# First cross attention of a six-layer stack: split q and k packed through DRAM for float32r score matmuls

## The chip, the cores and the metric

One core of a Trainium2 chip. The metric is the device time of the whole kernel in microseconds, the median of the runs shown.

## The reference, cut to what matters

64 sequences of 128 tokens and 128 channels pass through six layers: windowed attention, **cross attention with a memory**, routed experts, narrow attention, cross attention over pairs and a quantised feed-forward. Each layer adds its input and normalises. The change lies in the second layer:

```python
q = x @ Wq + bq                        # 128 x 128, 16 heads of 8
k = concat([fside @ Wk + bk, ctx])     # 128 + 120 keys
v = concat([fside @ Wv + bv, ctx])
attn = softmax(q k^T * 8 ** -0.5)      # per head, 128 x 248
out = (attn v) @ Wp + bp
x = layernorm(x + out)
```

(The reference concatenates the projected keys with `ctx_1024`; the kernel handles the 120 rows of `ctx_1024` and the 128 projected rows as two blocks of keys.)

## The kernel before, in words

The layers are stages in time, one block of engine programs each, with all engines meeting between them: `attend_window` (0 to about 478 us), `attend_keys_major` (478 to about 1130), `experts_sparse`, `attend_narrow`, `attend_pairs`. Everything here concerns `attend_keys_major`.

**Steps.** `pipeline` unrolls the first and last steps and loops over the middle. Step c works on sequences at different depths: SP loads for c+4 and c+3; PE transposes x and projects q, k, v for c+2 (`a`); ACT copies q and k out for c+1 (`b`), and POOL multiplies q with `quadmask` into `Qm` (L1732); PE computes the scores of c; the keys-major scores, exponentials and weighted sums belong to c-1 and c-2; c-3 to c-6 finish (normalisation, transposes, stores into `routed_x`, `routed_xT` and the logits). Most tiles are rings of four.

**The scores.** 16 heads lie as four groups of 32 partitions with four heads of 8 channels in each. To multiply one head with a 32-row contraction, `Qm` holds q four times, with only one head's channels kept in each copy. Scores are computed twice. In L1478 and L1489 ("across": queries by 248 keys, in banks S) they serve only the row maxima, which DVE takes with negation (L1625). In L1473 ("down": keys by four heads times 128 queries, 512 columns, in banks T) they get the negated maxima added by a bfloat16 matmul from `NB` (L1485), and ACT exponentiates them (L1577). `weigh` (L1504) multiplies with V, 32 small matmuls a call. Float32 matmuls appear in the trace as two passes each, so L1473 has two PE instructions for each line executed.

**Order on PE in step c**, which is written out by hand: `scores(c,0)`, `weigh(c-2,0)`, the transposes of the maxima through `diag` (L1523), `scores(c,1)`, transposes of x, xo and O (L1531, L1537, L1539, L1544), `scores(c,2)`, `weigh(c-2,1)`, `scores(c,3)`, transposes of OT and the projections (L1550, L1551, L1560 to L1564). Each call of `scores` is a round: two groups of down, two groups of across, on four different row groups, then two NB matmuls. Three banks each for S and T are reused within a step: round 1 needs the bank whose maxima DVE took in round 0.

**Other engines.** DVE, in order: normalisation of O (L1638 to L1645), V (L1414, L1415), y (L1656), two maxima, statistics, the copy of NB (L1665), two maxima, logits (L1675), xoT (L1679), oT (L1687), two maxima, xo (L1693), two maxima. ACT: q, k, two exponentials of 512 columns in each round, the copies of xT (L1598) and OT (L1603). POOL: the split of the maxima into three bfloat16 parts (L1719 to L1727), Qm, the context part of V (L1411, L1412), the power (L1742), yb (L1746). SP issues the seven transfers of a step in order (L1432 to L1449), with waits between them; it is one queue.

The stage before it ends with `slots<-blank` stores (L369, L389) that zero a DRAM area for the experts stage; before the change the stage doesn't wait for their landing.

Of the kernel before, what the change touches and what calls it, by code (L numbers as in the profile page):

```python
# [16 lines left out]
F32 = mybir.dt.float32  # L17
BF16 = mybir.dt.bfloat16
U32 = mybir.dt.uint32
# [4 lines left out]
P = 128  # L24
CTX = 120
WH = 8
# [14 lines left out]
BLANKS = 8  # L41

# [38 lines left out]
def looped(at):  # L81
    return not isinstance(at.p, int)

# [52 lines left out]
def allocate(K):  # L136
# [8 lines left out]
    K.alibi = K.sb("alibi", [P, WH * 48])  # L145
# [7 lines left out]
    K.blank = K.sb("blank", [P, BLANKS, ROW])  # L153
    K.half = K.sb("half", [P, 2])
    K.eps = K.sb("eps", [P, 1])
    K.Mself = K.sb("Mself", [P, WH * P])
    K.Nself = K.sb("Nself", [P, WH * P])
    K.Gram = K.sb("Gram", [P, 2 * P])
# [14 lines left out]
    K.tstep = K.sb("tstep", [P, 3])  # L173

# [84 lines left out]
def late_loads(K, D):  # L259

    return [
        (K.xw[:, 0, :], D["L0_xattn_Wq"]), (K.xw[:, 1, :], D["L0_xattn_Wk"]),
        (K.xw[:, 2, :], D["L0_xattn_Wv"]), (K.xw[:, 3, :], D["L0_xattn_Wp"]),
        (K.xb[:, 0:1], D["L0_xattn_bq"].rearrange("(d a) -> d a", a=1)),
        (K.xb[:, 1:2], D["L0_xattn_bk"].rearrange("(d a) -> d a", a=1)),
# [19 lines left out]
def attend_window(K, D, tag, x_dram, out_dram, nseq):  # L285
# [14 lines left out]
    with ExitStack() as ctx:  # L300
# [53 lines left out]
        with nc.Block() as block:  # L354
            @block.sync
            def _(sp):
# [972 lines left out]
def attend_keys_major(K, D, tag, x_dram, routed, nseq):  # L1329
# [6 lines left out]
    places = (slice(0, CTX), slice(CTX, CTX + P))  # L1336
# [6 lines left out]
    with ExitStack() as ctx:  # L1343
# [3 lines left out]
        def sem(name):  # L1347
# [6 lines left out]
        xf = [sb(f"xf{i}", [P, 2 * P + CTX + P]) for i in range(ring)]  # L1354
        qT = [sb(f"qT{i}", [P, P]) for i in range(2)]
        Qm = [sb(f"Qm{i}", [P, J * P]) for i in range(ring)]
# [24 lines left out]
        f_in = [sem(f"f_in{i}") for i in range(ring)]  # L1381
        xT_out = [sem(f"xT_out{i}") for i in range(ring)]
# [7 lines left out]
        cleared, ready, masked, put_ctx, split, maxed = (sem(n) for n in (  # L1390
            "cleared", "ready", "masked", "put_ctx", "split", "maxed"))
# [6 lines left out]
        cT, kT = slice(2 * P, 2 * P + CTX), slice(2 * P + CTX, 2 * P + CTX + P)  # L1398
        every = slice(2 * P, 2 * P + CTX + P)
# [24 lines left out]
        with nc.Block() as block:  # L1424
            @block.sync
            def _(sp):
                def step(c):
                    a, l, s, o = c + 4, c + 3, c, c - 5
                    if a.live:
# [3 lines left out]
                        sp.dma_start(cx[a.slot][0:CTX, :], D["ctx_1024"][a.n]).then_inc(x_in[a.slot], 16)  # L1433
                    if s.live:
# [11 lines left out]
                    if l.live:  # L1446
                        need(sp, T_ps, (l - 4).done(2 * R, 4))
# [120 lines left out]
            def _(act):  # L1568
# [11 lines left out]
                def step(c):  # L1580
# [11 lines left out]
                    if a.live:  # L1592
                        need(act, in_ps, a.done())
                        if n.live:
                            need(act, oT_ps, n.done())
# [656 lines left out]
```

## Time and profile before

| | us |
|---|---|
| runs (3) | 2698.47, 2702.93, 2707.09 |
| median | 2702.93 |
| profiled execution, span from first to last instruction | 2695.8 |
| profiled execution, its own time outside the span | not listed apart; the runs are 2.7 to 11.3 above the span |
| instructions | 95989 |
| PE busy in the span | 2502.7 (93%) |
| DVE, ACT, POOL busy | 1849.6, 1737.7, 1401.1 |

How to read it: PE is TensorE's matmuls and PEld its weight loads, DVE is VectorE, ACT ScalarE, POOL GpSimd, SP the engine that issues transfers (SPq its issues). The busy time of PE is an average over five stages. One step of the stage at hand is the time between two equal instructions of the loop.

### The profile page before, as it was taken

To read this page: it belongs to the slowest core of one execution; us is meant where nothing else is said; L and a number is where in the kernel's file an instruction comes from. 1 tells how busy PE (TensorE), PEld (TensorE's weight loads), DVE (VectorE), ACT (ScalarE), POOL (GpSimd) and SP (SyncE) were. 2 spreads that over 40 slices of the span, in tenths; PEclk is the share of its full clock that TensorE was granted. 3 is DMA by queue.
4 is the path that set the end of the run, shared out by engine and by line. 5 is a ranking of instruction groups with operands and counts; after the bars stand their busy time and mean duration, and the time that the engine had idled before them with its cause. 6 is when DMAs were issued, how large, how long until landed. Compare 5 with 4: busy or idle time off the path is not lost. (4 is left out here: it accounts for less than half of the span.)

```text
span 2695.8 us, 95989 instructions
## 1 busy us (share of the span) xinstructions
PE 2502.7 (93%) x29950; PEld 2007.2 (74%) x29951; DVE 1849.6 (69%) x5434; ACT 1737.7 (64%) x6375; POOL 1401.1 (52%) x2914
## 2 busy tenths in 40 slices
PE   7999999799999999788889969999999799999995
PEld 6888888577777777487667758888888688888883
DVE  4565555588888888564334448888887388888886
ACT  4666666355555555213556638888888588888883
POOL 2333333233444344165774447777776266666664
PEclk9999999799999999899999979999999899999997
DMA  6332322211111111123332211111111111111100
GB/s 158 100 88 79 89 81 65 65 49 48 49 48 48 48 47 44 37 85 84 78 80 66 66 48 53 47 53 49 50 53 37 33 31 32 31 31 31 31 26 11
DMA packets 270161, 151.37 MB, mean 56 GB/s; under 512 B 51776, under 2 KB 263744, under 8 KB 270016
## 3 DMA queue, kind: packets, MB, share of 16 engines
q1 hardware_dynamic: 261312, 131.57, 18.2%
q0 software_dynamic: 8704, 17.97, 1.9%
q8 instruction: 78, 1.28, 0.2%
q14 instruction: 67, 0.55, 0.1%
HBM read 92.52 MB, written 48.51 MB: 52 GB/s over the span
## 5 line engine op out<-in xcount | busy, mean ns | idle before, releaser
L1187 ACT ACTIVATE pr<-psS,small 128x128 f32<-128x128 f32 x1024 | 366.7, 384 | 95.9 <-DVE small L1258 94.0
L1625 DVE TENSOR_REDUCE small<-psS 128x2 f32<-128x496 f32 x512 | 321.4, 669 | 90.3 <-PE psS L1489 89.1
L1577 ACT ACTIVATE pr<-psT 120x512 f32<-120x512 f32 (+1 forms) x384 | 215.1, 595 | 136.9 <-PE psT L1485 124.5
L1473 PE MATMUL psT<-cross_Qm,cross_xf 32*120 32x512 f32 (+1 forms) x768 | 292.1, 641 | 0.5 <-ACT pr L1577 0.2
L1187 ACT ACTIVATION_READ_ACCUMULATOR pr<-psS,small 128x1 f32 x1024 | 226.1, 221 | 0.0
L1478 PE MATMUL psS<-cross_xf,cross_Qm 32*128 32x248 f32 x1024 | 209.1, 428 | 1.1 <-DVE small L1625 1.1
L2172 POOL DMA_INDIRECT results<-experts_ob,experts_xb x144 | 138.5, 962 | 115.4 <-ACT experts_ob L1992 100.5
L1258 DVE TENSOR_REDUCE small<-psS 128x8 f32<-128x1024 f32 x128 | 156.7, 1224 | 60.5 <-PE psS L1152 60.3
L2112 DVE SCALAR_TENSOR_TENSOR experts_bgh<-experts_bth,psS 128x256 f32<-128x256 f32 x144 | 60.7, 421 | 198.9 <-ACT experts_bth L1984 198.9
L956 POOL TENSOR_SCALAR pr<-pr,small 128x120 f32<-128x120 f32 x512 | 180.4, 372 | 23.3 <-DVE small L910 23.3
L814 ACT ACTIVATE pr<-psS,small 128x120 f32<-128x120 f32 x512 | 179.0, 391 | 5.0 <-DVE small L929 5.0
L1489 PE MATMUL psS<-cross_xf,cross_Qm 32*128 32x248 f32 x1024 | 181.4, 376 | 0.0
L484 ACT ACTIVATE pr<-pr,small 128x48 f32<-128x48 f32 x512 | 166.9, 331 | 2.9 <-DVE small L551 2.9
L1111 PE MATMUL psT<-ident,pr 128*128 128x128 f32 x1024 | 161.6, 281 | 0.2
L1152 PEld LDWEIGHTS psS<-self_qk,self_Qm 32*128 32x128 f32 x2048 | 125.7, 188 | 45.9 <-issue 45.9
L2163 POOL DMA_INDIRECT slots<-routed_x,experts_idx x128 | 123.6, 965 | 66.7 <-issue 38.1
L470 ACT COPY self_Y<-psW 128x512 f32<-128x512 f32 x128 | 68.7, 589 | 126.8 <-PE psW L456 126.8
L1152 PE MATMUL psS<-self_qk,self_Qm 32*128 32x128 f32 x2048 | 150.3, 285 | 0.0
L1473 PE MATMUL psS<-cross_Qm,cross_xf 32*120 32x512 f32 (+1 forms) x256 | 143.9, 642 | 0.0
L1504 PEld LDWEIGHTS psW<-pr,cross_Vx 120*32 120x32 f32 (+1 forms) x4096 | 104.0, 109 | 52.7 <-issue 51.8
L583 POOL TENSOR_TENSOR small<-small,eps 128x1 f32<-128x1 f32 x64 | 12.2, 191 | 249.0 <-DVE small L517 249.0
L1577 ACT ACTIVATE pr<-psS 120x512 f32<-120x512 f32 (+1 forms) x128 | 76.1, 595 | 98.9 <-PE psT L1485 98.9
(323 smaller groups left out, 8058.1 us busy)
## 6 DMA issues: line engine op xcount, KB each, us to landing
self_parts<-results SPq DMA_DIRECT2D x64, 192.0 KB, 2.4
slots<-blank SPq DMA_DIRECT2D x18, 520.0 KB, 4.5
experts_xb<-slots SPq DMA_DIRECT2D x144, 65.0 KB, 1.9
self_near<-in_x SPq DMA_DIRECT2D x128, 64.0 KB, 1.9
between<-self_xo SPq DMA_DIRECT2D x128, 64.0 KB, 1.6
cross_x<-between SPq DMA_DIRECT2D x128, 64.0 KB, 1.8
cross_res<-between SPq DMA_DIRECT2D x128, 64.0 KB, 1.8
self_x<-in_x SPq DMA_DIRECT2D x64, 64.0 KB, 1.8
```

Of the source, the lines that this page charges most:

```text
L484: last = act.activation(head(pr[e.slot], h), head(pr[e.slot], h), ACT.Exp, bias=nmax[e.slot % 2][:, h:h + 1], accum_out=tot[e.slot][:, h:h ...
L814: last = act.activation(pr[b.slot][:, i * P:i * P + CTX], S0[:, i * P:i * P + CTX], ACT.Exp, bias=nmax[b.slot % 2][:, i:i + 1], accum_out= ...
L956: last = pool.tensor_scalar(pr[w.slot][:, i * P:i * P + CTX], pr[w.slot][:, i * P:i * P + CTX], inv[w.slot][:, i:i + 1], 1.0, ALU.mult, AL ...
L1111: last = pe.transpose(W[half][:, n * P:(n + 1) * P], pr[t.slot % 4][:, (4 * half + n) * P:(4 * half + n + 1) * P], K.ident[:])
L1152: last = pe.matmul(K.S[u.slot % 2][:, 512 * half + m * P:512 * half + (m + 1) * P], Qm[i.slot % 2][rows(g), m * P:(m + 1) * P], qk[i.slot] ...
L1187: last = act.activation(pr[e.slot % 4][:, cols], K.S[e.slot % 2][:, cols], ACT.Exp, bias=nmax[e.slot % 4][:, n:n + 1], accum_out=tot[k.slo ...
L1258: dve.tensor_reduce(nmax[u.slot % 4][:], src, AX.X, ALU.max, negate=True).then_inc(maxed, 1)
L1473: pe.matmul(to[0:size, :], xf[t.slot][rows(g), every][:, places[ck]], Qm[t.slot][rows(g), :], start=True, stop=False)
L1478: pe.matmul(to[:, 0:CTX + P], Qm[c.slot][rows(g), P * j0:P * j0 + P], xf[c.slot][rows(g), every], start=True, stop=True)
L1489: pe.matmul(to[:, 256:256 + CTX + P], Qm[c.slot][rows(g), P * j0 + P:P * j0 + 2 * P], xf[c.slot][rows(g), every], start=True, stop=True).t ...
L1577: act.activation(PT[k][0:sizes[ck], 512 * n:512 * n + 512], T[turn[2 * r + n]][0:sizes[ck], :], ACT.Exp).then_inc(exped, 1)
L1625: dve.tensor_reduce(nmax[c.slot % 2][:, J * sg[n] + j0:J * sg[n] + j0 + 2], src, AX.X, ALU.max, negate=True).then_inc(maxed, 1)
```

## The change

What it does:

- q and k get a channel order by place in the head group (`t_xq`, `t_xk`, `t_bq`, `t_bk`, `t_ctxq` prepared on the host). ACT writes q and k, and a transfer the context, into `low` (128 x 376). DVE keeps the upper bits in `high` (one `bitwise_and` over 376 columns), POOL subtracts `high` from `low`.
- SP stores high and low in four transfers to a DRAM tensor `parts` (four combinations of high and low q with high and low k), waits for all of them to land, and loads `pack` (128 x 4 x 376) from it. In `pack` the 32 rows of a group hold, for each of four heads, 8 channels in the four combinations. `Qm`, `qT`, `quadmask`'s multiply and the load of `t_ctx` are gone.
- The scores read `pack` as float32r: across is still two matmuls of 248 columns a group and round, down is four of 128 columns with weights of their own in place of one of 512.
- NB, xoT, oT and the logits are copied by ACT, xo is computed by POOL; DVE did all five.
- Projections run one step earlier (a = c+3), q and k are copied out at h = c+2; V's projection is at c+2.
- `keep_awake` issues unread 512-column float32 matmuls: six before the first wait of the stage, and in the unrolled steps up to sequence 1 two or six at the start of a step and one in its middle.
- The stage before now waits for all `slots<-blank` stores, and some of its tiles are freed at its end.

Core of the diff:

```diff
 (SP)
-                    if l.live:
-                        need(sp, T_ps, (l - 4).done(2 * R, 4))
-                        sp.dma_start(xf[l.slot][:, P:2 * P], D["t_fside"][l.n]).then_inc(f_in[l.slot], 16)
-                        sp.dma_start(xf[l.slot][:, cT], D["t_ctx"][l.n]).then_inc(f_in[l.slot], 16)
+                        need(sp, v_ps, (a - 4).done())
+                        sp.dma_start(xf[a.slot][:, P:2 * P], D["t_fside"][a.n]).then_inc(f_in[a.slot], 16)
+                    if l.live:
+                        need(sp, parts_out[(l - 2).slot], (l - 2).p * STORES + STORES)
+                        sp.dma_start(low[l.slot % 2][:, 2 * P:], D["t_ctxq"][l.n]).then_inc(c_in[l.slot], 16)
...
+                    if h.live:
+                        need(sp, low_sb, h.done())
+                        to = K.parts[h.slot].rearrange("n p k -> p n k")
+                        mine = part[h.slot % 2]
+                        sp.dma_start(to[:, 0:4:3, :], mine[:]).then_inc(parts_out[h.slot], 16)
+                        sp.dma_start(to[:, 1:3, queries], mine[:, :, queries]).then_inc(parts_out[h.slot], 16)
+                        sp.dma_start(to[:, 1, keys], mine[:, 1, keys]).then_inc(parts_out[h.slot], 16)
+                        sp.dma_start(to[:, 2, keys], mine[:, 0, keys]).then_inc(parts_out[h.slot], 16)
+                        need(sp, T_ps, (h - 4).done(2 * R))
+                        need(sp, parts_out[h.slot], h.p * STORES + STORES)
+                        sp.dma_start(pack[h.slot][:].rearrange("p j k -> p (j k)"),
+                                     K.parts[h.slot].rearrange("n (s j) k -> s n (j k)", j=J)).then_inc(
+                            pack_in[h.slot], 16)
 (PE)
+                wide = K.xw[:, 0:4, :].rearrange("p n d -> p (n d)")
+                keep_awake(pe, W1, K.ident[:], wide, 6)
...
+                    def down(n, j):
+                        if t.live:
+                            g, to = tg[n], T[turn[2 * r + n]]
+                            pe.matmul(to[0:size, P * j:P * j + P], pack[t.slot][rows(g), j, places[ck]].bitcast(F32R),
+                                      pack[t.slot][rows(g), j, queries].bitcast(F32R), start=(j == 0), stop=False)
+                    def across(n, j):
+                        if c.live:
+                            g, to = sg[n], S[turn[2 * r + n]]
+                            last = pe.matmul(to[:, 256 * j:256 * j + CTX + P], pack[c.slot][rows(g), j0 + j, queries].bitcast(F32R),
+                                             pack[c.slot][rows(g), j0 + j, keys].bitcast(F32R), start=True, stop=True)
...
-                            pe.matmul(to[0:size, :], xf[t.slot][rows(g), every][:, places[ck]], Qm[t.slot][rows(g), :],
-                                      start=True, stop=False)
...
+                    filling = not looped(c) and c.n < 2
+                    if filling and not c.live:
+                        keep_awake(pe, W1, K.ident[:], wide, 2)
+                    if filling and c.live and not m.live:
+                        keep_awake(pe, W1, K.ident[:], wide, 6)
...
+                    if filling:
+                        keep_awake(pe, W1, K.ident[:], wide, 1)
 (DVE, at the start of a step, ahead of the first maxima)
+                    if h.live:
+                        need(dve, qk_sb, h.done(2))
+                        need(dve, c_in[h.slot], h.landed())
+                        need(dve, parts_out[c.slot], c.p * STORES + STORES)
+                        dve.tensor_scalar(high[h.slot % 2].bitcast(U32), low[h.slot % 2].bitcast(U32), UPPER, None,
+                                          ALU.bitwise_and).then_inc(top_sb, 1)
 (POOL)
-                        pool.tensor_tensor(Qm[b.slot][:].rearrange("p (j q) -> p j q", j=J),
-                                           qT[b.slot % 2][:].rearrange("p (j q) -> p j q", j=1).to_broadcast([P, J, P]),
-                                           K.quadmask[:].rearrange("p (j q) -> p j q", q=1).to_broadcast([P, J, P]),
-                                           ALU.mult).then_inc(masked, 1)
+                    if h.live:
+                        need(pool, top_sb, h.done())
+                        pool.tensor_tensor(low[h.slot % 2], low[h.slot % 2], high[h.slot % 2],
+                                           ALU.subtract).then_inc(low_sb, 1)
 (stage before, SP)
+                sp.wait_ge(K.emptied, 16 * empty.shape[0])
```

## Rows read from the trace of the kernel before

**Rows 1.** Page: the span.

```profile
span 2695.8 us, 95989 instructions
```

**Rows 2.** Windows: filling, then steady steps: length; PE, PEld, DVE, ACT, POOL; clock, DMA share, GB/s.

```profile
480.00:540.00 60.00, 53.54 (x509) 37.28 (x510) 33.82 (x88) 20.88 (x49) 16.08 (x47) 0.75 0.18 43
...
560.00:656.50 96.50, 96.50 (x1428) 68.42 (x1427) 79.27 (x228) 55.98 (x124) 39.23 (x116) 1.00 0.18 49
```

**Rows 3.** Instruction groups, forms apart, 560 to 1090 us: busy, mean ns, idle.

```profile
L1625 DVE TENSOR_REDUCE small<-psS 128x2 f32<-128x496 f32 x448 | 281.0, 669 | 69.4 <-PE psS L1489 68.9
...
L1577 ACT ACTIVATE pr<-psT 128x512 f32<-128x512 f32 x168 | 93.9, 594 | 31.8 <-PE psT L1485 31.8
L1732 POOL TENSOR_TENSOR cross_Qm<-cross_qT,quadmask 128x512 f32<-128x512 f32 x56 | 58.3, 1041 | 0.1
...
L1665 DVE CAST cross_NB<-psW 128x512 bf16<-128x512 f32 x56 | 38.7, 691 | 4.2
```

**Rows 4.** Timeline of PE over one step: start us, us, instruction.

```profile
706.44 0.69 PE L1473 MATMUL psT<-cross_Qm,cross_xf 32*120 32x512 f32 x1
...
707.79 1.08 PE L1504 MATMUL psW<-pr,cross_Vx 128*32 128x128 f32 x32
...
708.80 0.69 PE L1473 MATMUL psT<-cross_Qm,cross_xf 32*120 32x512 f32 x1
...
710.08 0.33 PE L1550 MATMUL psW<-ident,cross_OT 128*128 128x128 f32 x1
...
711.34 0.69 PE L1473 MATMUL psT<-cross_Qm,cross_xf 32*128 32x512 f32 x1
...
712.62 1.08 PE L1504 MATMUL psW<-pr,cross_Vx 120*32 120x128 f32 x32
...
713.63 0.40 PE L1523 MATMUL psW<-identb,cross_diag 128*128 128x128 bf16 x4
...
713.96 0.69 PE L1473 MATMUL psS<-cross_Qm,cross_xf 32*128 32x512 f32 x1
...
715.24 0.33 PE L1531 MATMUL psW<-ident,cross_x 128*128 128x128 f32 x1
```

**Rows 5.** Timeline of PE inside the round from 713.96: second pass, then NB.

```profile
714.49 0.59 PE L1473 MATMUL psS<-cross_Qm,cross_xf 32*128 32x512 f32 x1
...
714.92 0.37 PE L1485 MATMUL psS<-cross_NB,cross_onesb 32*128 32x512 bf16 x1
```

**Rows 6.** Timeline of PE: float32 matmuls of 128 columns, two passes each.

```profile
710.35 0.39 PE L1560 MATMUL psW<-cross_xf,xw 128*128 128x128 f32 x2
...
710.58 0.39 PE L1561 MATMUL psW<-cross_xf,xw 128*128 128x128 f32 x2
```

**Rows 7.** Timeline of SP: first and last of a step's seven issues.

```profile
710.24 0.34 SPq L1448 DMA_DIRECT2D cross_xf<-in_t_fside  x1
...
713.56 0.51 SPq L1444 DMA_DIRECT2D routed_x<-cross_xo  x1
```

**Rows 8.** DMA issues: count, KB each, median us from issue to landing.

```profile
slots<-blank SPq DMA_DIRECT2D x18, 520.0 KB, 4.5
...
between<-self_xo SPq DMA_DIRECT2D x128, 64.0 KB, 1.6
...
wT<-in_t_wq SPq DMA_DIRECT2D x1, 512.0 KB, 3.6
```

**Rows 9.** Windows of one us around the stage's start, columns as in Rows 2.

```profile
474.00:475.00 1.00, 0.00 (x0) 0.00 (x0) 0.00 (x0) 0.00 (x0) 0.00 (x0) 0.50 1.02 377
...
482.00:483.00 1.00, 0.00 (x0) 0.00 (x0) 0.62 (x17) 0.00 (x0) 0.25 (x2) 0.50 0.92 204
```

**Rows 10.** Timeline of the filling: stage's first memset, first scores, third sequence's.

```profile
478.12 0.91 DVE L1610 MEMSET cross_Vx<- 128x1024 f32 x1 [6.13 <-PEq L354]
...
489.48 1.20 PE L1478 MATMUL psS<-cross_xf,cross_Qm 32*128 32x248 f32 x4
...
511.95 0.69 PE L1473 MATMUL psT<-cross_Qm,cross_xf 32*128 32x512 f32 x1
```

More of the change, by code:

```diff
@@ L17 @@
 F32 = mybir.dt.float32
+F32R = mybir.dt.float32r
 BF16 = mybir.dt.bfloat16
@@ L82, in looped, with keep_awake @@
     return not isinstance(at.p, int)
+def keep_awake(pe, bank, weights, moving, times):
+    for _ in range(times):
+        pe.matmul(bank, weights, moving, start=True, stop=True)
 def pipeline(eng, step, ring, count, first, lo, hi, last):
@@ L173, in allocate @@
     K.tstep = K.sb("tstep", [P, 3])
+    K.alibi = K.sb("alibi", [P, WH * 48], F32, early)
+    K.Mself = K.sb("Mself", [P, WH * P], F32, early)
+    K.Nself = K.sb("Nself", [P, WH * P], F32, early)
+    K.Gram = K.sb("Gram", [P, 2 * P], F32, early)
+    K.blank = K.sb("blank", [P, BLANKS, ROW], F32, early)
 def set_up(K, D):
@@ L1352, in attend_keys_major @@
         res = [sb(f"res{i}", [P, P]) for i in range(ring)]
-        xf = [sb(f"xf{i}", [P, 2 * P + CTX + P]) for i in range(ring)]
-        qT = [sb(f"qT{i}", [P, P]) for i in range(2)]
-        Qm = [sb(f"Qm{i}", [P, J * P]) for i in range(ring)]
+        xf = [sb(f"xf{i}", [P, 2 * P]) for i in range(ring)]
+        part = [sb(f"part{i}", [P, 2, WIDE]) for i in range(2)]
+        high, low = ([v[:, i, :] for v in part] for i in range(2))
+        pack = [sb(f"pack{i}", [P, J, WIDE]) for i in range(ring)]
         Vx = [sb(f"Vx{i}", [P, 2, G, P]) for i in range(ring)]
@@ L1381, in attend_keys_major @@
         f_in = [sem(f"f_in{i}") for i in range(ring)]
+        c_in = [sem(f"c_in{i}") for i in range(ring)]
+        parts_out = [sem(f"parts_out{i}") for i in range(ring)]
+        pack_in = [sem(f"pack_in{i}") for i in range(ring)]
+        top_sb, low_sb, v_ps = sem("top_sb"), sem("low_sb"), sem("v_ps")
         xT_out = [sem(f"xT_out{i}") for i in range(ring)]
@@ L1389, in attend_keys_major @@
             "in_sb", "qk_sb", "v_sb", "nb_sb", "exped", "O_sb", "oT_sb"))
-        cleared, ready, masked, put_ctx, split, maxed = (sem(n) for n in (
-            "cleared", "ready", "masked", "put_ctx", "split", "maxed"))
+        cleared, ready, put_ctx, split, maxed = (sem(n) for n in (
+            "cleared", "ready", "put_ctx", "split", "maxed"))
         inverted, scaled = sem("inverted"), sem("scaled")
@@ L1553, in step @@
                         need(pe, in_sb, a.done())
-                        need(pe, f_in[a.slot], a.p * 32 + 32)
+                        need(pe, f_in[a.slot], a.landed())
                     if n.live:
@@ L1596, in step @@
[L1596 to L1597 removed]
                         act.copy(xf[a.slot][:, 0:P], W0[:, 0:P]).then_inc(in_sb, 1)
+                    if n.live:
+                        need(act, y_ps, (n - 2).done())
+                        act.copy(oT[n.slot % 2][:], W0[:, 384:512]).then_inc(oT_sb, 1)
+                    if v.live:
+                        act.copy(routed.logits[:, bass.ds(v.n, 1), :].rearrange("p a e -> p (a e)"), W0[:, 256:256 + EXPERTS])
@@ L1599, in step @@
+                    if z.live:
+                        need(act, xT_out[z.slot], (z - 4).landed())
+                        act.copy(xoT[z.slot][:], W0[:, P:2 * P]).then_inc(turned_sb, 1)
                     exps(c, 2)
@@ L1742, in step @@
                         pool.tensor_tensor(rs[w.slot % 2][:], ve[w.slot % 2][:], K.half[:, 0:1], ALU.pow).then_inc(lnroot, 1)
+                        need(pool, lnroot, w.done())
+                        need(pool, stored[w.slot], (w - 4).landed())
+                        need(pool, turned_ps, (w - 4).done())
                     if v.live:
```

139 lines of the change are left out of this document (65 added, 74 removed).

## The prediction

> **What bounds the kernel now.** I read the windows first. In a stretch of 96.5 us (10.2 steps of 9.46) PE is busy 96.50 of 96.50 us at full clock, DVE 79.27, ACT 55.98, POOL 39.23, and DMA 18% at 49 GB/s [rows 2]. The reader is to see that in the steady part only PE has no slack. The groups give the step: 448 maxima, eight a step, are 56 steps in 530 us, 9.46 us each [rows 3]. The timeline of PE cuts that step. Three rounds of scores take 1.28 us and one 1.35 (706.44 to 707.79), in all 5.19. The rest is two `weigh` of 1.01, diag 0.33, the transposes 0.66 (715.24 to 706.44 plus one step) and the tail 1.26 from 710.08 to 711.34: 4.27, and 9.46 with the rounds [rows 4]. The change attacks the 5.19. The stage fills from 478.12, computes its first scores at 489.48 and those of the third sequence at 511.95 [rows 10], at a mean clock of 0.75 [rows 2].
>
> **PE after the change.** A round's first pass starts at 713.96, the second 0.53 later, NB 0.43 after that, and the next work 0.32 later [rows 4, 5]. So a 512-column float32 pass streams in 0.43, with 0.10 to start a round. The four row groups run side by side, so the down groups, which also carry NB, set the length; across is two matmuls of 248 columns and fits beside them. New is: 0.10 + four matmuls of 128 columns with weights of their own + 0.32 for NB and the turn to the next work. No row has float32r. The nearest below is bfloat16: four diag matmuls of 128 columns in 0.33, 0.083 each [rows 4]. The nearest above that is one float32 pass: L1560's two passes take 0.23, some 0.11 each [rows 6]. The far end is both passes, 0.22 to 0.23. The round is 0.75, 0.86 or 1.32 us, and the step on PE 4.27 + 4 x round = 7.3, 7.7 or 9.5. I take one float32 pass, 7.7, because the operands are 32 bits wide and it is one pass.
>
> **The other engines.** DVE sheds NB, 0.69 [rows 3], and four smaller copies, and gains one bitwise operation over 376 columns ahead of its first maxima: from 7.77 a step (79.27 / 10.2 [rows 2]) it stays below 7.7 even if that costs 0.6, NB alone counted. It delays the first maxima; round 1 of PE needs their bank, and may wait some 0.3 us, so PE stands near 8.0. ACT gains NB (about the 0.59 of an exponential of the same size [rows 3]) and three copies, together about 1.3: 5.5 [rows 2] becomes 6.8. POOL, 3.85 [rows 2], loses 1.04 for Qm's 512 columns [rows 3] and gains a subtraction over 376 and xo over 128, each less than that: under 4.9. So these cost nothing while PE or SP takes 7.7 us or more.
>
> **SP and the transfers.** This is the new path. Per step SP issues seven small transfers as before (x, cx, fside, ctxq, res, xT, xo), then waits for POOL's `low`, issues four stores of 752 KB together, waits until they have landed, and issues the 752 KB load. Nothing passes the wait: x, fside and the next sequence's stores are queued behind it. The seven issues take 3.83 us today, from 710.24 to 714.07 [rows 7]. The pack's issue is another 0.5. The landing: a 64 KB store to DRAM takes 1.6, 512 KB inward 3.6, and 520 KB of blanks 4.5 in a busy stretch [rows 8]; full engines moved 377 GB/s [rows 9]. From the first issue, 1.6 + 688 KB at 377 GB/s (1.9) is 3.5 at the low end; by the blanks' slope, 2.9 us for 456 KB, it is 1.6 + 4.4 = 6.0 at the high end. I take 4.0, nearer the low one, because the rows stored here are mostly 1 to 1.5 KB long and the engines are else little used. So SP's turn is 3.83 + 4.0 + 0.5 = 8.3 us, with ends of 7.8 and 10.3. The load itself has a step and a half until it is needed, so its 3 to 4 us are hidden; if SP falls behind, that cover is gone and SP's turn is the step. 1.5 MB more per step at 377 GB/s is 4.1 us of 8.3: the engines are not full.
>
> The Trainium skill ("DMA: Bandwidth & Descriptors", Anatomy of one DMA) fits a transfer on its GpSimd path as about 2.0 us plus bytes over 436 GB/s, most of the fixed part being the receipt from the target. By that the stores would land 3.8 us after the first issue, SP's turn would be 8.1 and the total below 13 us lower; no row here shows it for this queue.
>
> **Step and steady gain.** The step is the longest of PE 8.0 and SP 8.3: 8.3. Over some 62 steps (64 less the filling) 62 x (9.46 - 8.3) = 72 us saved. The drain has score work too: 2 us more.
>
> **Filling.** First, the stage before now waits for its blank stores. DMA engines are still 92% busy up to 483 [rows 9], where the stage had begun at 478.12 [rows 10]: up to 4.9 us later. Second, the unread matmuls stand ahead of the first transpose: six of two passes are 5.2 us warm (12 x 0.43) and 10.3 at half clock. Third, the first scores now wait for copy, split, stores and load, about 8 us more. I expect first scores some 18 us later than 489.48. But the next steps were slow before, 22.5 us for two (489.48 to 511.95 [rows 10]), and come at SP's pace, 16.6, from there, some at full clock. The third sequence starts about 12 us later than before; less 3 for what the blanks would have delayed anyway, 9. Bounds are 3 and 18.
>
> Sum: 72 + 2 - 9 = 65 us off the span of 2695.8 [rows 1], 2631. The median of the runs shown stands 7.1 above that span, so **2638**.
>
> **The rivals.**
> 1. *The round trip is shorter and PE decides* (chance 0.20). SP issues at its best and the stores land in 3.5; DVE's wait stays hidden. PE's row-based 7.3 to 7.7 sets the step, say 7.5: 62 x 1.96 + 2 - 9 = 115, 2588. For it: a load's issue itself takes 0.34 [rows 7], and at 0.45 from issue to issue SP's turn is 3.2 + 3.5 + 0.5 = 7.2. Against: the spacing is 0.55 today (3.83 / 7), and the stage has DVE waits within a step.
> 2. *float32r at short columns is no cheaper than two float32 passes*, so that the change doesn't do what it says (0.08). No matmul here has 256 columns. The round is 1.32, the step 9.5, and only the filling remains: 2703 + 7, some 2710. For it: no row excludes it. Against: one pass issued in place of two.
> 3. *Slower: SP waits for its stores longer than 5.1 us.* That is the point at which its turn reaches 9.46. At the blanks' slope the landing is 6.0, the step 10.3: 62 x 0.84 + 7 = 59 more, 2762 (0.12). For it: 520 KB took 4.5 [rows 8], four stores plus a write receipt each step, and the loads in flight share the engines. Against: the blanks are 520-byte rows beside a stage at up to twice this stage's traffic.
> 4. *A step of 8.8 to 9.4*, the same mechanism short of the turning point (0.10): 2670 to 2706.
>
> **How the numbers follow.** The forecast, a step of 7.9 to 8.8, has 0.50, and its own range is 2613 to 2669. About 0.3% (8 us, 2695 to 2711) is what a measurement here can tell from no change. Faster takes the forecast, rival 1 and most of rival 4, 0.79. Within: most of rival 2 and the edge of rival 4, 0.07. Slower: rival 3 and the rest of rival 2, 0.14. The range of 2582 to 2706 takes in rival 1 and rival 4 and leaves out rival 3 and most of rival 2.
>
> **What would show it.** In the trace after: L1473's successor with one PE instruction a matmul, four in 0.33 to 0.46; rounds near 0.86; PE under 100% busy in steady steps, and its idle time ended by the landing of `pack` if SP decides, by DVE's maxima at round 1 if it doesn't. SP's own queue should wait 2 us after the fourth store. The steps between equal maxima should be 8.3. DMA share should rise from 0.18 to above 0.6. The first scores should stand 15 to 20 us later. The prediction is wrong if float32r matmuls of 128 columns start 0.2 us apart, if the stores land after 5.1 us, or if the step is set by ACT, whose copies now stand between its exponentials.

## The result and the profile after

The change makes the kernel slower: 2821.34 us median of four runs (2802.70 to 2857.34) against 2700.70 before, a ratio of 1.0424 with a 95% interval of 1.0386 to 1.0462. The prediction was 2638 (2582 to 2706). The profiled execution took 2802.7 us, its span is 2800.9, against a span of 2695.8 before [rows 1]. Ratios in this document leave out runs over 1.5% above the fastest of their kernel (here 2857.34), so they differ a little from the quotient of the medians.

The page of the kernel after: the span, then PE's busy tenths, the granted clock and the DMA share in 40 slices of 70 us.

```profile
span 2800.9 us, 96503 instructions
PE   7999997999999999869888987999999799999995
PEclk9999999768755557989999998999999999999997
DMA  6323232566644445622333221111111111111100
```

The reader is to see the clock's row: from the 8th to the 16th slice, all of them in the first cross attention, it stands at 5 to 8 tenths, while PE's row shows 9 tenths busy in every one. PE is not short of work there, it runs at half clock. The windows of the stage say it more closely (length; PE, PEld, DVE, ACT and POOL busy; clock, DMA share, GB/s):

```profile
660.00:699.00 39.00, 38.82 (x697) 29.77 (x696) 32.35 (x91) 31.93 (x81) 22.96 (x60) 1.00 0.70 214
700.00:730.00 30.00, 25.89 (x471) 19.92 (x471) 21.92 (x60) 20.64 (x52) 15.36 (x40) 1.00 0.71 225
760.00:1060.00 300.00, 300.00 (x3072) 223.21 (x3068) 147.46 (x397) 145.34 (x353) 100.88 (x264) 0.50 0.47 149
```

These are the three paces of the stage, where before there was one [rows 2]. I take the pace from the distance between POOL's subtractions, one a step. From 660 to 699 PE is full at full clock: 7.76 us a step. From 700 to 730 PE is 86% busy at full clock: 8.5 to 9.6 us. From 760 to 1060 PE is full at 0.50, which is 1.2 GHz: 13.6 us. In this execution 33 steps behind the first scores take 12.8 us or more, in stretches of 2, 5 and 26 (the first 2 are in the filling, where the kernel before had slow steps too).

Between the second and the third pace stands this, in windows of 2 us:

```profile
726.00:728.00 2.00, 0.46 (x8) 0.28 (x7) 0.94 (x6) 0.66 (x3) 1.25 (x5) 1.00 1.02 360
728.00:730.00 2.00, 2.00 (x54) 1.47 (x51) 1.29 (x3) 1.09 (x2) 0.85 (x1) 1.00 0.78 262
...
736.00:738.00 2.00, 1.20 (x22) 0.97 (x26) 0.79 (x4) 0.44 (x3) 0.71 (x3) 0.95 0.82 245
738.00:740.00 2.00, 2.00 (x36) 1.50 (x28) 1.51 (x4) 0.90 (x2) 1.34 (x3) 0.50 0.98 331
```

and in the timeline of PE the wait that empties the first of them:

```profile
727.73 0.32 PE L1502 MATMUL psT<-cross_pack 32*128 32x128 f32 x1 [1.54 <-DMA cross_pack<-parts]
```

PE stands for `pack` 1.54 us before 727.73 and again 1.34 before 736.80; then the clock is at half. The earlier fall, at about 588, has a wait of 1.53 us before 585.76 in front of it.

SP's own timeline shows why `pack` is late (one turn, from pack load to pack load; L1472 and L1475 are the first and last store, L1478 the load):

```profile
723.27 0.57 SPq L1478 DMA_DIRECT2D cross_pack<-parts  x1
724.18 0.34 SPq L1449 DMA_DIRECT2D cross_x<-between  x1
...
727.38 0.50 SPq L1466 DMA_DIRECT2D routed_x<-cross_xo  x1
727.99 0.52 SPq L1472 DMA_DIRECT2D parts<-cross_part  x1
...
729.62 0.46 SPq L1475 DMA_DIRECT2D parts<-cross_part  x1
732.15 0.57 SPq L1478 DMA_DIRECT2D cross_pack<-parts  x1
```

The turn is 8.88 us; every fourth is some 0.9 longer, and the eight from 659.58 to 732.15 take 9.07 on average. SP issues almost without a pause to 730.08 and then stands 2.07 us until the stores have landed. A PE that needs 7.76 us a step overtakes it. During a stretch of 13.6 us a step it is the other way round: SP gets ahead, its turns stretch to 13.6 too, and once the clock is back PE finds `pack` ready for about five steps at its own pace of 7.76 before it waits again.

The loss has two parts. The last maxima of the stage start at 1217.0, before at 1098.9: 118 us later. How much of that is the clock? The maxima of the fifth sequence start at 554.6 (before: 532.6). If each of the 59 steps from there took SP's 9.07 us, those of the last sequence would start at 554.6 + 59 x 9.07 = 1090; in the kernel before they start at 1091.1. This is an estimate, and experiment 4 comes near it: with a clock of 0.97 they start at 1092.8. So without a fall behind the filling the change would about break even, and the falls cost some 120 us. SP's turn has by then taken what float32r saves.

### The profile page after: what moved, and what is told of

It reads as the page before. It is cut to its first block and busy times, and to the rows that moved or that the text cites. A ratio compares the mean times of both kernels' runs of the same rounds, so it can differ in the third digit from the quotient of the medians.

```text
span 2800.9 us, 96503 instructions
## 1 busy us (share of the span) xinstructions
PE 2572.2 (92%) x29876; PEld 2090.5 (75%) x30003; DVE 1773.6 (63%) x5178; ACT 1800.0 (64%) x6631; POOL 1448.8 (52%) x2978
## 5 line engine op out<-in xcount | busy, mean ns | idle before, releaser
L1502 PE MATMUL psT<-cross_pack 32*120 32x128 f32 (+1 forms) x1536 | 231.9, 354 | 21.7 <-DMA cross_pack<-parts 20.5
L1502 PEld LDWEIGHTS psT<-cross_pack 32*120 32x120 f32 (+1 forms) x1536 | 186.8, 248 | 70.8 <-issue 48.7
L1550 PE MATMUL psW<-pr,cross_Vx 120*32 120x128 f32 (+1 forms) x4096 | 194.1, 350 | 0.6 <-ACT pr L1632 0.6
L1508 PE MATMUL psS<-cross_pack 32*128 32x248 f32 x1024 | 179.4, 416 | 3.4 <-DVE small L1692 1.8
L1550 PEld LDWEIGHTS psW<-pr,cross_Vx 120*32 120x32 f32 (+1 forms) x4096 | 141.3, 139 | 49.8 <-issue 42.6
L454 PE MATMUL psT<-Nself,self_Y 128*128 128x128 f32 x1024 | 131.2, 282 | 3.5 <-ACT self_Y L481 3.5
```

Source lines behind the costliest of these rows:

```text
L1502: pe.matmul(to[0:size, P * j:P * j + P], pack[t.slot][rows(g), j, places[ck]].bitcast(F32R), pack[t.slot][rows(g), j, queries].bitcast(F32 ...
L1508: last = pe.matmul(to[:, 256 * j:256 * j + CTX + P], pack[c.slot][rows(g), j0 + j, queries].bitcast(F32R), pack[c.slot][rows(g), j0 + j, k ...
L1550: last = pe.matmul(W1[rows(g), cols], Vx[t.slot][0:size, ck, g, 32 * j:32 * j + 32], PT[2 * ck + g // 2][0:size, 512 * (g % 2) + P * j:512 ...
```

## The experiments

Theory: float32r brings what it should, but PE then waits for `pack`, a wait of over a microsecond drops its clock to half, and at half clock the one-pass matmuls keep it there for many steps. Rivals: the transfers as such cost the time; float32r lowers the clock without any wait; the copies moved to ACT hold PE up.

Each experiment ran beside runs of the kernel before on the same chip. In 1 to 8 and in 12 the experts stage behind this one takes some 115 us longer for every kernel, the one before too (its medians there are 2816.17, 2817.29 and 2812.55); in 9 to 11 the kernel before is at 2698.30. So absolute times are read as ratios, and the stage by its own trace. The first window below is the kernel after's, from 600 to 1040 us; the others are those of the experiments over the same stretch, in the order in which they come.

```profile
600.00:1040.00 440.00, 433.90 (x5052) 325.16 (x5049) 241.14 (x653) 237.18 (x579) 166.45 (x435) 0.60 0.53 167
```

**1. Float32 in place of float32r.**

```diff
-pack[t.slot][rows(g), j, places[ck]].bitcast(F32R), pack[t.slot][rows(g), j, queries].bitcast(F32R)
+pack[t.slot][rows(g), j, places[ck]], pack[t.slot][rows(g), j, queries]
...
-pack[c.slot][rows(g), j0 + j, queries].bitcast(F32R), pack[c.slot][rows(g), j0 + j, keys].bitcast(F32R)
+pack[c.slot][rows(g), j0 + j, queries], pack[c.slot][rows(g), j0 + j, keys]
```

> The kernel after with the four float32r views of pack taken away: the same tiles are multiplied as float32, two passes each; stores, pack load, moved copies and unread matmuls stay. Clock theory (the loss is PE at half clock for some 350 us, and PE falls there because one-pass matmuls finish early and PE then stands idle for pack): PE needs 4.27 + 4 x 1.32 = 9.5 us a step, more than SP's turn of 8.6 to 9, so it never waits for pack, the clock stays at 1.00 in steady steps, and the time is 2705 to 2725. Rival (transfers and their waits as such cost the time): SP's turn is unchanged, the time stays above 2790.

Measured: 2834.93 against 2816.17 before, ratio 1.0063 (1.0040 to 1.0086). The expected 2705 to 2725 was meant beside a kernel before at 2703; as a ratio it is 1.001 to 1.008, and held. Window:

```profile
600.00:1040.00 440.00, 440.00 (x8632) 348.46 (x8626) 303.35 (x829) 299.20 (x738) 212.19 (x554) 1.00 0.66 209
```

Same stores and loads, DMA busier than in after (0.66), clock 1.00, steps of 9.5 to 9.6 us. So the same transfers cost little while PE's step is longer than SP's turn. The extra time of this kernel is the later filling (first maxima at 513.4, before at 491.5) and some 0.08 us a step.

**2. Only the five moved operations**, put into the kernel before: four copies from DVE to ACT, `xo` from DVE to POOL. Two of the five:

```diff
-dve.tensor_copy(NB[m.slot % 2][:], W0[:]).then_inc(nb_sb, 1)
+act.copy(NB[m.slot % 2][:], W0[:]).then_inc(nb_sb, 1)
...
-dve.tensor_copy(oT[n.slot % 2][:], W0[:, 384:512]).then_inc(oT_sb, 1)
+act.copy(oT[n.slot % 2][:], W0[:, 384:512]).then_inc(oT_sb, 1)
```

> The kernel before with only the five small operations moved: NB, xoT, oT and the logits copied by ACT, xo computed by POOL. My step budget: PE bounds the step with 9.46 us, DVE falls from 7.8 to about 6 and ACT rises to 6.8, so nothing changes: within 0.3% of before. Rival (ACT's copies between its exponentials hold up PE's transposes): slower by over 0.3%.

Measured: ratio 0.9996 (0.9983 to 1.0009), as expected. The moves cost and bring nothing while PE sets the step.

**3. The pack load one step later**, ahead of SP's wait for `low` and the stores of the step, so that SP needn't wait for stores that it has just issued. The load of `ctxq` goes with it, to the place just before.

```diff
+                    g = c + 1
+                    if g.live:
+                        need(sp, T_ps, (g - 4).done(2 * R))
+                        need(sp, parts_out[g.slot], g.p * STORES + STORES)
+                        sp.dma_start(pack[g.slot][:].rearrange("p j k -> p (j k)"),
...
                     if h.live:
                         need(sp, low_sb, h.done())
...
-                        need(sp, T_ps, (h - 4).done(2 * R))
-                        need(sp, parts_out[h.slot], h.p * STORES + STORES)
-                        sp.dma_start(pack[h.slot][:].rearrange("p j k -> p (j k)"),
```

> The kernel after with one edit on SP: the load of pack for sequence c+1 is issued ahead of the wait for low of c+2, one step after its stores, so SP no longer stands waiting for stores to land (its turn falls from 8.6 to about 6.5 us). Clock theory: PE is never short of pack, each steady step takes the 7.76 us of the fast stretches, the clock stays at 1.00, and the time is 2590 to 2630. Rival (float32r matmuls on 32 rows work the array so little that the clock falls without any gap): half-clock stretches of 13.6 us a step remain, and the time stays above 2720.

Measured: 2898.7 (2807.13 to 2917.64) against 2816.17; the runs lie too far apart for a ratio with an interval. The expectation failed. The load no longer waits for SP, but it is issued 5 us before it is needed and shares the engines with the stores behind it; it takes 5.3 us to land in the full-clock part (4.7 in after). In the profiled execution, that of 2917.64, a wait of 1.64 us before 585.28 is followed by 28 steps at half clock. When the clock is back, four steps take 7.8 and the next ones 8.0 to 8.9, most with a wait of 0.4 to 1.0 us, and there is no fall from those. The next fall stands behind a wait of 3.73 before 1185.00. This doesn't decide between the theory and its rival.

**4. One unread matmul of 512 columns in each looped step**, ahead of the wait for `pack`.

```diff
                     if c.live and r == 0:
+                        if looped(c):
+                            need(pe, exped, (c - 2).done(2 * R, 3))
+                            keep_awake(pe, T[turn[0]], K.ident[:], wide, 1)
                         need(pe, pack_in[c.slot], c.landed())
```

> The kernel after with one unread float32 matmul of 512 columns (two passes, 0.86 us at full clock) in each looped step, ahead of PE's wait for pack; its result is overwritten. Clock theory: it fills most of the gap of 0.8 to 1.5 us in which PE waits for pack, so the clock falls seldom or not at all; steps are 8.6 to 9 us and the time 2640 to 2690. Rival (thin activity): the clock still falls, with half-clock steps now of 13.6 + 1.7 us, and the time is above 2820.

Measured: 2819.10, ratio 0.9986 (0.9961 to 1.0010); expected as a ratio was 0.977 to 0.995, a miss. The clock was nearly full all the same:

```profile
600.00:1040.00 440.00, 424.15 (x6769) 304.15 (x6768) 319.37 (x865) 307.93 (x768) 220.72 (x577) 0.97 0.69 219
```

Waits of up to 3.00 us remain near the filling, where SP's turns are 9.5 to 11.1 us and its stores land 5.1 to 5.9 us after the first issue; later a turn takes 9.05 on average, and so does nearly every step once SP's lead is used up (9.02 from 733.6 to 850.9). The clock falls three times, behind waits of 3.00, 1.31 and 2.36. The first two falls cost one slow step each (14.14 and 13.97), where after had 5 and 26; the third lasts over the last two steps (11.71 and 12.37). All eight runs lie within 24 us, and a stretch of 15 steps would add some 15 x (13.6 - 9.0) = 69, so it is unlikely that any had one. The stretches are short in this kernel, and still it only breaks even with the kernel before: the time that float32r saves goes to waits for `pack`.

**5. SP's stores first in its step**, behind the load of `ctxq`; the small issues stand between them and the pack load, which stays where it was.

```diff
                 def step(c):
                     a, l, s, o, h = c + 4, c + 3, c, c - 5, c + 2
+                    if l.live:
+                        need(sp, parts_out[(l - 2).slot], (l - 2).p * STORES + STORES)
+                        sp.dma_start(low[l.slot % 2][:, 2 * P:], D["t_ctxq"][l.n]).then_inc(c_in[l.slot], 16)
+                    if h.live:
+                        need(sp, low_sb, h.done())
+                        to = K.parts[h.slot].rearrange("n p k -> p n k")
+                        mine = part[h.slot % 2]
+                        sp.dma_start(to[:, 0:4:3, :], mine[:]).then_inc(parts_out[h.slot], 16)
...
                     if h.live:
-                        need(sp, low_sb, h.done())
-                        to = K.parts[h.slot].rearrange("n p k -> p n k")
...
                         need(sp, T_ps, (h - 4).done(2 * R))
                         need(sp, parts_out[h.slot], h.p * STORES + STORES)
```

> The kernel after with SP's order in a step changed: context load, wait for low, four stores, then x, cx, fside, res, xT, xo, and the pack load last. The six small issues now stand between the stores and the wait for their landing, so SP's turn is about 6.5 us instead of 8.6, and pack still has over one step until it is needed. Gap theory (the clock falls where PE stands 0.8 to 1.5 us for pack): steady steps take 7.76 us without gaps; half-clock stretches begin in the filling alone, and are left once; the stage ends 60 us or more before that of after (last maxima at 1217), near 1040 to 1150. Rival (float32r's short matmuls let the clock fall without a gap): falls from full clock in the middle of steady 7.76 us steps.

Measured: 2864.06 (2764.14 to 2881.36) against 2817.29, again too far apart for an interval; the fastest run is 53 us below before, the others 30 to 64 above. In the profiled one, that of 2847.29, the last maxima start at 1138.4, within the expected. The steps are 7.8 (every other one 8.2 to 8.8 late in the stage). But in the steady part a wait for `pack` remained and the clock fell there, in windows of 4 us and in the timeline of PE:

```profile
606.00:610.00 4.00, 3.38 (x60) 2.52 (x58) 3.04 (x9) 3.35 (x10) 2.63 (x7) 1.00 0.67 202
610.00:614.00 4.00, 3.05 (x54) 2.25 (x54) 2.37 (x7) 1.26 (x3) 1.98 (x6) 0.79 0.86 270
614.00:618.00 4.00, 4.00 (x37) 2.79 (x37) 1.96 (x5) 2.34 (x7) 1.69 (x4) 0.50 0.53 130
```

```profile
610.95 0.32 PE L1503 MATMUL psT<-cross_pack 32*128 32x128 f32 x1 [1.57 <-DMA cross_pack<-parts]
```

Then 15 steps of 13.6 us in which PE waits for nothing:

```profile
640.00:800.00 160.00, 160.00 (x1634) 119.03 (x1626) 78.33 (x211) 77.49 (x188) 53.99 (x143) 0.50 0.47 149
```

Once the clock is back at 813.68 there are ten waits for `pack` of 0.50 to 0.75 us. Nine of them bring nothing. The first is followed by a wait for another transfer, `cx`, whose load stands behind the stores in this order and took 4.99 us to land here (median of the loop 2.55). In the timeline of PE and in windows of 4 us:

```profile
868.85 0.32 PE L1503 MATMUL psT<-cross_pack 32*128 32x128 f32 x1 [0.50 <-DMA cross_pack<-parts]
873.35 0.33 PE L1584 MATMUL psW<-ident,cross_x 128*128 128x128 f32 x1 [1.21 <-DMA cross_cx<-in_ctx]
```

```profile
872.00:876.00 4.00, 2.79 (x45) 2.20 (x47) 2.38 (x5) 2.69 (x8) 1.99 (x4) 0.89 0.53 133
876.00:880.00 4.00, 4.00 (x52) 3.05 (x43) 1.88 (x6) 1.78 (x5) 0.88 (x4) 0.68 1.00 335
```

The clock falls at 875.12 and is back at 878.53; the step takes 11.22 us. The last fall stands behind a wait of 2.49 at 1114.71. The expectation of a clock at 1.00 failed. The rival that lowers it without any wait has no case here: from 878.53 to 1114 all-float32r steps run at full clock. But it isn't waits either that keep the clock low for 15 steps.

**6. Only the across matmuls back to float32, SP as in after.**

```diff
-pack[c.slot][rows(g), j0 + j, queries].bitcast(F32R), pack[c.slot][rows(g), j0 + j, keys].bitcast(F32R)
+pack[c.slot][rows(g), j0 + j, queries], pack[c.slot][rows(g), j0 + j, keys]
```

> The kernel after with the across matmuls as float32 (two passes of 248 columns), down still float32r. A round is then about 0.10 + 4 x 0.21 + 0.32 = 1.2 us at most, so the step is 8.3 to 9.1 us against SP's 8.6: small gaps stay. If one-pass matmuls keep a half clock for long because they work the array little, half-clock stretches are much shorter than the 29 steps of after, and the last maxima come before 1150. If the number of passes doesn't matter, the stretches are as long as in after.

Measured: 2806.28, ratio 0.9968 (0.9947 to 0.9989). Last maxima at 1101.1. A wait of 1.90 us, longer than any that started a long stretch in after, brings the clock down, and it is back 10 us later, after one step of 13.8:

```profile
604.00:608.00 4.00, 2.10 (x27) 1.91 (x28) 2.32 (x9) 1.71 (x4) 1.26 (x5) 1.00 0.88 285
608.00:612.00 4.00, 4.00 (x58) 2.77 (x55) 1.72 (x4) 1.67 (x3) 1.35 (x3) 0.51 0.59 196
...
616.00:620.00 4.00, 4.00 (x60) 3.16 (x59) 2.04 (x4) 2.14 (x5) 0.59 (x1) 0.71 0.74 247
620.00:624.00 4.00, 4.00 (x77) 2.94 (x77) 3.28 (x12) 2.71 (x6) 2.70 (x8) 1.00 0.59 198
```

Twelve later waits of 0.52 to 0.92 us bring no fall. So a wait lowers the clock in either form. That the clock comes back sooner with more two-pass matmuls is likely from this run, not shown by its one fall: falls that cost a single slow step also occur with all scores in one pass (experiments 5, 8 and 9). What speaks for it here is that all seven runs lie within 18 us, where four of the kernel after spread over 55. Experiment 12 shows it better.

**7. Both: stores first and across in float32**, the edits of 5 and of 6 together.

> Both edits: SP's order with the stores first, and the across matmuls as float32. No gap (SP's turn 6.5 us against a PE step of 8.3 to 9.1) and more work on the array: full clock in all steady steps, last maxima at 1050 to 1095, and the whole kernel faster than before on the same chip by 0 to 50 us.

Measured: 2786.41, ratio 0.9896 (0.9874 to 0.9917), 31 us faster than before; last maxima at 1079.1, all as expected. No wait for `pack` over 0.5 us, no fall:

```profile
600.00:1040.00 440.00, 440.00 (x7693) 336.55 (x7696) 328.10 (x897) 321.63 (x794) 230.83 (x596) 1.00 0.72 225
```

The step is 8.86 us.

**8. After without any unread matmul.**

```diff
 def keep_awake(pe, bank, weights, moving, times):
 
-    for _ in range(times):
-        pe.matmul(bank, weights, moving, start=True, stop=True)
+    return
```

> The kernel after without any unread matmul. If they serve their purpose, the filling is at half clock for longer and the float32r steps start at half clock and stay there: last maxima later than 1217 or about there. If they only cost time, the first scores come 10 us earlier and the rest is as in after.

Measured: ratio 1.0419 (1.0358 to 1.0480); first maxima at 501.6 instead of 510.5, last at 1206.3; stretches of 2, 7, 21 and 1 slow steps. The filling's unread matmuls cost some 9 us at the first scores and show no benefit. Since after itself comes out between 1.02 and 1.04, a small effect either way could not be seen here.

**9. The kernel after again**, unchanged.

> The kernel after, unchanged, on the chip of these experiments (where the experts stage of every kernel takes about 110 us longer). Gap theory: each half-clock stretch starts behind a wait for pack of 1.3 us or more and its length is chance, so the executions differ by several per cent, and the stage's last maxima come some 60 to 130 us later than those of before. If the half clock belonged to the first chip alone, all executions would be near each other and faster than before.

Measured: 2772.85 (2747.64 to 2807.19) against 2698.30, ratio 1.0222 (1.0165 to 1.0280). The long experts stage that the expectation took for granted is absent here, although the record gives these runs the same chip number as experiments 1 to 4; what brings those 115 us is open. Last maxima at 1178.4, 80 us later than before and within the expected; stretches of 2, 19, 1, 3 and 1 slow steps. The loss is there in both sets of runs, and its size varies from run to run: these runs lie 49 to 109 us above the kernel before, the four of the first result 102 to 157 above its 2700.70.

**10. As 7, without the unread matmuls of the filling**, by the edit of 8.

> Stores first, across as float32, and no unread matmuls in the filling. The first scores come about 10 us earlier but at half clock. With two of three passes back, steps at half clock should end within a few steps by themselves, as in the kernel before: equal to the version with unread matmuls within 10 us, or up to 10 us faster. If the unread matmuls are needed, a long half-clock stretch appears and it is over 40 us slower.

Measured: 2672.23 against 2698.30, ratio 0.9899 (0.9876 to 0.9922), the same as 7 and as expected. With two-pass matmuls among the scores, unread matmuls in the filling bring nothing.

**11. Stores first (the edit of 5), all float32r, one unread matmul of 256 columns in each looped step.**

```diff
+                        if looped(c):
+                            need(pe, exped, (c - 2).done(2 * R, 3))
+                            keep_awake(pe, T[turn[0]][:, 0:256], K.ident[:], wide[:, 0:256], 1)
```

> Stores first, all scores in float32r, and one unread float32 matmul of 256 columns (two passes, 0.43 us) in each looped step ahead of the wait for pack. The step is 7.8 + 0.45 = 8.2 to 8.3 us, above what SP and the transfers need (7.8 to 8.5), so gaps are 0.3 us at most. If the half clock is kept by little work, this adds some and stretches get shorter than the 15 to 17 steps without it; if one gap near the filling (1.57 us at 611) still comes, a stretch of several steps follows. Whole kernel between 2740 (no stretch) and 2820.

Measured: 2662.42 (2649.40 to 2671.07), ratio 0.9847 (0.9814 to 0.9880). The expected 2740 to 2820 was meant beside a kernel before at 2817; as a ratio it is 0.973 to 1.001, and held. From 627 on, steps are 8.0 to 8.5 us, most of them 8.0 to 8.1. But seven steps from 532 to 627, in the filling's tail, take 12.7 to 14.4, and the clock is back only at 626.83, after the first two unread matmuls of the loop. A last fall, at 1063.74, stands behind waits of 1.72 and 1.09 us.

**12. As 11, with the across matmuls in float32 in the unrolled steps and float32r in the loop.**

```diff
-                            last = pe.matmul(to[:, 256 * j:256 * j + CTX + P], pack[c.slot][rows(g), j0 + j, queries].bitcast(F32R),
-                                             pack[c.slot][rows(g), j0 + j, keys].bitcast(F32R), start=True, stop=True)
+                            q, k = pack[c.slot][rows(g), j0 + j, queries], pack[c.slot][rows(g), j0 + j, keys]
+                            if looped(c):
+                                q, k = q.bitcast(F32R), k.bitcast(F32R)
+                            last = pe.matmul(to[:, 256 * j:256 * j + CTX + P], q, k, start=True, stop=True)
```

> Stores first and one unread matmul of 256 columns in each looped step, as in the run before, but the across matmuls are float32 in the unrolled steps (up to sequence 7 and the last ones) and float32r in the loop. In the run before, eight steps behind the filling took 13.2 to 14.4 us at half clock. If two passes let the clock rise early, those steps take about 8.9 instead and the looped ones 8.0 to 8.1: 25 to 40 us less than the run before, some 0.975 of the kernel before. If the clock falls at the change to float32r without a gap, a half-clock stretch appears at about 590 us and nothing is gained.

Measured: 2751.61 against 2812.55, ratio 0.9780 (0.9752 to 0.9808). Expected was some 0.975, and 25 to 40 us less than the run before; the last maxima start at 1046.1 against 1073.1, 27 less, with the first at 515.4 against 515.2. (The slow steps behind that run's filling are seven, not eight as the expectation counts them.) The same window of experiment 11, then windows of the filling's tail and of the loop in this one:

```profile
560.00:600.00 40.00, 40.00 (x416) 29.62 (x412) 19.89 (x55) 19.28 (x45) 13.69 (x37) 0.50 0.47 146
560.00:600.00 40.00, 40.00 (x699) 30.32 (x700) 30.06 (x84) 28.97 (x71) 21.77 (x57) 1.00 0.70 213
700.00:1000.00 300.00, 299.72 (x5240) 226.89 (x5236) 245.28 (x670) 238.55 (x598) 170.03 (x446) 1.00 0.83 246
```

PE is full in both first windows, and only the across matmuls differ between the two kernels. After the filling's fall the clock is at half for 17 us here (522.53 to 539.60) and for 106 us with across in one pass (521.02 to 626.83). The two other pairs that differ in across alone go the same way in the filling, by the granted clock from 500 to 585 us: 38 us at half in the kernel after against 20 in experiment 6, and 55 in experiment 5 against 3 in experiment 7. So with two-pass across matmuls the clock comes back sooner; each of these times is from one execution. The clock does not fall at the change to float32r. This version beats the kernel before by 2.2% and the kernel after by more.

## Why the prediction was wrong, step by step

**The step that failed** is "The step is the longest of PE 8.0 and SP 8.3: 8.3". It let PE stand idle for the difference at no cost but the difference. The text even named the sign, "PE under 100% busy in steady steps, and its idle time ended by the landing of `pack` if SP decides", as what would show it right. What the runs show in its place: an idle time of 1.2 us or more can take the clock to 1.2 GHz, and the step then is 13.6 us for 1 to 28 steps. No rival had the clock. The falls cost some 120 us, an estimate from the sum above; it is more than the whole forecast gain of 65.

Both numbers in that step were off as well, and they widened the gap between them. PE needs 7.76 (predicted 8.0) and SP 9.07 us (predicted 8.3), so PE stands idle some 1.3 us a step where the prediction had 0.3 (0.85 to 1.54 in the waits from 700 to 737). In no run does a fall in steady steps stand behind waits of 0.3 us alone, so at the predicted sizes the clock might have held; that isn't shown.

The slower side was given 0.14, most of it for SP waiting over 5.1 us for its stores. In the full-clock steady steps the stores land 4.1 to 4.2 us after the first issue. Right behind the filling, and in front of the first long stretch, two turns have 5.8 and 5.1 (from 559.86 and 570.88), so that rival may have had a part in where the first fall came. Its step of 10.3 didn't come.

**The terms that were mis-sized**:
- *SP's turn of 8.3.* Measured 9.07 on average: 0.77 us more, and over 62 steps 48 of the 72 us saved are gone. In the turn shown above (8.88), first store to pack load is 4.16 us (727.99 to 732.15), predicted 4.0; the pack's issue and the seven small ones take 4.72 (723.27 to 727.99), predicted 0.5 and 3.83. The average is higher than 8.88 because one turn in four is longer.
- The fit of the Trainium skill ("DMA: Bandwidth & Descriptors", Anatomy of one DMA) gave 3.8 for the landing, for another queue; the measured 4.16 decides.
- *The filling.* First scores 18 us later were predicted; the first maxima start at 510.5 instead of 491.5, 19 later. But the next steps did not come at SP's pace: two of them took 12.7 and 13.5 at half clock, and the fifth sequence is 22 us later than before, where the sum had 9.

**The terms that held**, all at full clock:
- *A float32r matmul of 128 columns costs one float32 pass, 0.11.* In the timeline of PE of the kernel after, round 1 of a step:

```profile
662.57 0.32 PE L1502 MATMUL psS<-cross_pack 32*128 32x128 f32 x1
...
662.85 0.32 PE L1502 MATMUL psS<-cross_pack 32*128 32x128 f32 x1
...
663.01 0.27 PE L1502 MATMUL psS<-cross_pack 32*128 32x128 f32 x1
...
663.12 0.27 PE L1502 MATMUL psS<-cross_pack 32*128 32x128 f32 x1
...
663.56 0.33 PE L1583 MATMUL psW<-ident,cross_x 128*128 128x128 f32 x1
```

 The last two stand 0.11 apart. The 0.28 between the first two is the predicted wait of round 1 for its bank's maxima ("may wait some 0.3 us"). The round takes 0.99, the other three 0.78 to 0.88, and the step 7.76 (predicted 7.7, 8.0 with the wait). Rival 2, no gain from short columns, is out.
- *The other engines.* The copies moved to ACT and POOL cost nothing (experiment 2).

The total does not belong to them. At full clock and with its own order on SP the kernel after would save nothing by the estimate above, and experiment 4, nearly at full clock, has 0.9986. The 61 us that experiment 12 saves, near the 65 predicted, come with another order on SP and a step of 8.0 to 8.5, and with a matmul that nothing reads; that the two numbers are close is luck.

What stays open: why the clock is back after 5 steps in one stretch and 26 in another of one execution, with the same instructions at the same pace; and why waits of 1.99, 2.08 and 2.47 us late in the stage (before 1165.08, 1192.40 and 1210.23 of the kernel after) brought no fall before its end. In front of every fall in steady steps stands a wait of 1.21 us or more, directly or one step before (that of 1.21 had one of 0.50 four us before it), and none of the some 60 waits for `pack` of 0.5 to 1.2 us is followed by a fall by itself; of the waits from 1.2 to 2.5, some are and some aren't. A wait put into the kernel before on purpose wasn't tried.

## What to carry to other kernels

An engine that becomes faster than its supply doesn't merely wait: on TensorE a wait of little more than a microsecond can cost the clock (here every fall in steady steps had a wait of 1.2 us or more in front of it), so a matmul saving is only safe with its operands ahead of need. The supply's turn has to be read over several steps, since here one in four is longer, and it caps the gain even where the clock holds (experiment 4). The order of one SP queue (stores first, small issues between, dependent load last) made the steps shorter, but was not enough alone (experiment 5); with across in two passes, or with a small unread matmul in each looped step, it was (experiments 7, 11 and 12). After a fall, look whether the matmuls that remain are enough to bring the clock back; keeping some of them in two passes was cheaper here than losing it. And where runs of one program spread by several per cent, read the granted clock by stretches before any engine's busy time: PE was 99 to 100% busy both at 7.76 and at 13.6 us a step.

## What the runs showed of the hardware that was not expected

- PE stayed at 1.2 GHz for 26 steps, 353 us, while it was busy 300.00 of 300.00 us in the window from 760 to 1060. Being "busy" in the profile was not enough to lift the clock. The Trainium skill ("TensorE: Matmul & The Clock Gate", HAM oscillation — how this bites in real kernels) describes matmuls that go to half clock behind waits for a DMA, and its remedy is a loop that does its matmuls together before it waits for a DMA, so that PE stays warm. The first half agrees with the trace (1.54 and 1.34 us of wait, then 0.50). The remedy agrees as far as no fall came without a wait (experiments 7 and 12); but once the clock was down, 300 us without a wait did not bring it back in these one-pass steps.
- Waits of much the same length, 1.5 to 1.9 us, are followed by 26, 15, 28 and, in experiment 9, by 1 slow step with all scores in one pass. With only down in one pass the one fall (1.90) cost 1 (experiment 6), and in the filling two-pass across matmuls ended the half clock after 17 us instead of 106 (experiments 11 and 12).
- One unread matmul of 256 columns a step, 0.43 us of about 8, goes with no slow step in the loop behind its first, where the same kernel without it had 15 in a row; its four runs lie within 22 us, those without it within 117 (experiments 5 and 11). That it was the extra work and not the smaller wait is only likely: both changed.
